# Index tables built from chunk tails: four graph layers on one core of a Trainium2

## The reference

```python
msgs = feature[edge_src]; neigh = segment_sum(msgs, edge_dst)                      # layer 0
h = relu((feature + neigh) @ W1 + b1); out = h @ W2 + b2
scores = einsum('ehd,ehd->eh', q[src], k[tgt]) / sqrt(16) + edges @ We + be        # layer 1
scores = scores * cons[tgt] + relu(distances @ Wd1 + bd1) @ Wd2 + bd2              # softmax over each tgt
agg = segment_sum(x[src], dst); out = self and neighbour products                  # layer 2
agg = segment_sum(edge_weight[:, None] * x[src], dst); out = agg @ W + b           # layer 3
```

## Time and profile before

| | |
|---|---|
| median of three runs | 5493.49 us |
| span of the profiled execution | 5523.1 us |
| first stage, to the barrier | about 0 to 549 us of the span |
| edge batches in it | 49 |
| TensorE busy, whole span | 4522.1 us (82%) |
| VectorE (DVE) busy, whole span | 3190.2 us (58%) |

### The profile page before, as it was taken

How to read it: one execution, slowest core, us unless ns; L and a number is a source line. 1 busy time by engine, 2 the same in 40 slices (tenths; PEclk the granted TensorE clock), 3 DMA queues, 4 the chain that set the end, 5 groups by cost and what they waited for, 6 DMA issues and landing times. The chain is left out here.

```text
span 5523.1 us, 87967 instructions
## 1 busy us (share of the span) xinstructions
PE 4522.1 (82%) x25332; PEld 3171.9 (57%) x25333; DVE 3190.2 (58%) x4531; ACT 1790.6 (32%) x3407; POOL 2040.8 (37%) x1926
## 2 busy tenths in 40 slices
PE   6988665566899968888888888888885499999999
PEld 4656332222788844545555455455543388888888
DVE  6423988877211058988898899989885620000000
ACT  2433367889100030122333344445552410001000
POOL 0320035200000007777777777777775310000000
PEclk9989998988999989999999999999996599999999
DMA  8885567655766643444555566666665566669998
GB/s 182 177 166 123 117 232 277 267 247 241 303 279 279 279 136 81 118 133 139 152 156 169 160 181 185 186 194 195 197 198 149 203 264 279 279 254 297 299 294 264
DMA packets 736811, 1150.50 MB, mean 208 GB/s; under 512 B 310074, under 2 KB 659454, under 8 KB 717888
## 3 DMA queue, kind: packets, MB, share of 16 engines
q1 hardware_dynamic: 461601, 653.45, 34.8%
q10 hardware_dynamic: 211504, 349.71, 18.2%
q0 software_dynamic: 63600, 146.16, 10.6%
HBM read 762.49 MB, written 393.26 MB: 209 GB/s over the span
## 5 line engine op out<-in xcount | busy, mean ns | idle before, releaser
L1518 POOL DMA_INDIRECT at_qg<-q_d,at_slot x1616 | 1676.4, 1037 | 495.8 <-issue 492.4
L713 PE MATMUL bw_ps<-bw_mov,bw_sta 128*128 128x392 bf16 x7056 | 1576.4, 346 | 20.4 <-issue 8.0
L1060 PE MATMUL at_p3t<-tiles,h 128*128 128x256 f32 (+1 forms) x4900 | 1048.5, 376 | 6.2 <-ACT h L915 5.9
L1060 PEld LDWEIGHTS at_p3t<-tiles,h 128*128 128x128 f32 x4900 | 914.0, 191 | 127.1 <-issue 6.1
L1561 PE MATMUL at_psk<-at_kp,at_hot 128*128 x4848 | 615.2, 233 | 357.7 <-DVE at_qg L1639 302.2
L713 PEld LDWEIGHTS bw_ps<-bw_mov,bw_sta 128*128 128x128 bf16 x7056 | 631.8, 101 | 371.3 <-issue 104.4
L1561 PEld LDWEIGHTS at_psk<-at_kp,at_hot 128*128 128x128 bf16 x4848 | 436.3, 100 | 704.7 <-issue 498.1
L713 PE MATMUL ba_ps<-ba_mov,ba_sta 128*128 128x392 bf16 x2352 | 510.4, 363 | 321.3 <-ACT ba_ps L672 126.9
L676 DVE TENSOR_TENSOR ba_mov<-iota,key 128x3136 bf16<-128x3136 f16 x294 | 526.8, 1792 | 131.7 <-PE ba_ps L713 126.9
L713 PEld LDWEIGHTS ba_ps<-ba_mov,ba_sta 128*128 128x128 bf16 x2352 | 241.5, 103 | 590.2 <-issue 474.3
L697 DVE TENSOR_TENSOR bw_sta<-bw_raw,kw 128x1024 bf16<-128x1024 bf16 x882 | 557.4, 687 | 0.0
(11 more groups left out here) (409 smaller groups left out, 3536.1 us busy)
## 6 DMA issues: line engine op xcount, KB each, us to landing
adj_d<-ba_stage ACTq DMA_DIRECT2D x49, 3136.0 KB, 8.9
l0adjt<-adj_d SPq DMA_DIRECT2D x23, 6272.0 KB, 17.3
tiles<-adw_d SPq DMA_DIRECT2D x23, 6272.0 KB, 20.4
tiles<-adj_d SPq DMA_DIRECT2D x22, 6272.0 KB, 17.4
adw_d<-xall ACTq DMA_DIRECT2D x65, 1568.0 KB
adw_d<-bw_stage ACTq DMA_DIRECT2D x33, 1568.0 KB
at_rel<-rel_d SPq DMA_DIRECT2D x101, 512.0 KB
at_qg<-q_d,at_slot POOLq DMA_INDIRECT x1616
```

What stands on the lines that cost most here:

```text
L713: ins = pe.matmul(self.ps[:, bass.DynSlice(place, WCOL)], self.sta[:, k, u // 2, :, u % 2], self.mov[:, u // 2, :, u % 2], start=False, st ...
L1060: ins = pe.matmul(ps_agg[par][:, 0:n * P], h[:, hi, :], moving[hi], start=hi == 0, stop=hi == NB - 1 and not own_term, skip_group_check=ow ...
L1518: pool.indirect_dma_start(out=qg[:, ring, b, :], out_offset=None, in_=q_d[:, :], in_offset=bass.IndirectOffsetOnAxis(ap=slot[:, ring, b:b ...
```

## The change

The three tables are copied from the inputs in DRAM to DRAM by 13 transfers on ACT's queue, ahead of the edge loads there; POOL writes the padding. `rows_d` now has three planes as int32. SP loads the targets once more, and from the last element of each row DVE makes three 0/1 tables, whose products on TensorE count, for each node, the rows that end below it. The windows of all visits come from a second such count. All this stands ahead of batch 0 in TensorE's queue. The gathers of visits and of `KeyTables` follow at once. The visits' keys are made in five groups of up to four columns; `KeyTables.finish` and its stores (now on POOL) follow batches 4 to 7, two more planes and the weights are turned next, and batches 8 to 11 follow. The exact beginnings of the nodes (49 gathers) come last of the index work, and batches 12 to 48 behind them.

```diff
+def index_loads(nc, c, src, dst, edge_weight, x):
 ...
+    x.tails_here = c.L.dma(sp.dma_start(x.tail_row[:, 0:nf, :], dst[0:nf * P * P].rearrange("(g p e) -> p g e", p=P, e=P)))
 ...
+    for k, a in enumerate((dst, src, edge_weight.bitcast(I32))):
+        act.dma_start(c.rows_d[0:whole, k, :], a[0:whole * P].rearrange("(r e) -> r e", e=P)).then_inc(x.s_tables, 16)
 ...
+    for k, a in enumerate((dst, src)):
+        act.dma_start(c.ends_d[0:whole, k * P:(k + 1) * P], a[0:whole * P].rearrange("(r e) -> r e", e=P)).then_inc(x.s_tables, 16)
 ...
+    act.dma_start(c.dst_d[0:whole, :], dst[0:whole * P].rearrange("(r e) -> r e", e=P)).then_inc(x.s_tables, 16)
 ...
+        for k in range(CG):
+            T(pe.matmul(ps[:, 0, 0:NB], over[:, k, :], here[:, k, :], start=k == 0, stop=False))
+            t = T(pe.matmul(ps[:, 0, 0:NB], ones[:], under[:, k, :], start=False, stop=k == CG - 1))
 ...
+        wait(pool, visits)
+        pool.wait_ge(x.s_tables, x.to_tables)
+        wait(pool, x.padded)
+        for i in range(VG):
+            pool.indirect_dma_start(out=vis[:, i, :, :]..., in_=c.rows_d..., ...).then_inc(s_got[i // GV], 16)
 ...
+        keys.places()
+        keys.gather()
 ...
+        edges.batches(0, 4)
 ...
+        for q, i0 in enumerate(range(0, VG, GV)):
+            ve.wait_ge(s_got[q], 16 * n)
+            chain(tensor_tensor d = target - 8 * window, tensor_scalar hi = source >> 7)
+            chain(tensor_scalar o, scalar_tensor_tensor l, scalar_tensor_tensor k)
+            chain(scalar_tensor_tensor o)
+            m = chain(scalar_tensor_tensor k)
+            wait(pe, m)
+            b0, t0 = turn(k, n)
+            b1, t1 = turn(l, n)
+            read(c.key, i0, n, b0, t0, -1.0)
+            read(c.lo, i0, n, b1, t1, 0.0)
+        wait(pe, (V.sem, V.n))
+        edges.batches(4, 8)
+        stored = keys.finish()
+
+        wait(ve, stored)
+        chain(ve.tensor_scalar(hf[:], srcs, 0.5, 1.0 / WCOL, ALU.add, ALU.mult))
         for step in (-0.5, ROUND, -ROUND):
+            chain(ve.tensor_scalar(hf[:], hf[:], step, None, ALU.add))
+        chain(scalar_tensor_tensor dl)
+        chain(scalar_tensor_tensor k2, scalar_tensor_tensor hf)
+        wait(pe, (V.sem, V.n))
+        for what, dest, shift in ((k2, c.kw[:, 0, :], -1.0), (hf, c.lo2, 0.0), (weights, wc, 0.0)):
+            for i0 in range(0, VG, GV):
+                b, t = turn(what[:, i0:i0 + n, :], n)
+                read(dest, i0, n, b, t, shift)
 ...
+        edges.batches(8, 12)
+
+        m = chain(ve.tensor_copy(full_i[:], full[:]))
+        wait(pool, m)
         for j in range(NB):
-            a = V(ve.tensor_scalar(junk[:], heads[:], nodeid[:, j:j + 1], None, ALU.is_lt, ALU.add, accum_out=cnt[:, j:j + 1]))
-            wait(ve, a)
 ...
+            ld = c.Q.dma(pool.indirect_dma_start(out=ends[:, j, :], out_offset=None, in_=c.dst_d[:, :], ...))
+        wait(ve, ld)
+        for j0, j1 in ((0, 25), (25, NB)):
+            chain(ve.tensor_tensor(r, ends[:, j0:j1, :], nodeid[:, j0:j1]..., ALU.is_lt))
+            chain(ve.tensor_reduce(some[:, j0:j1], r, AX.X, ALU.add))
+        m = chain(scalar_tensor_tensor c.rp)
+        wait(pe, m)
         T(pe.matmul(ps[:, 0, 0:NB], c.shift, c.rp[:, 0:NB], start=True, stop=False))
 ...
-        edges.batches(40, EBATCH - 1 - ER)
+        edges.batches(12, EBATCH - 1 - ER)
         edges.last_batches()
         nc.all_engine_barrier()
 ...
+    def finish(self):
+        wait(ve, self.got)
+        m = chain(ve.tensor_copy(rel, ends[:, :, P:2 * P]))
+        wait(pe, m, self.ready)
+        (13 transposes, 8 products on TensorE; DVE reads them into c.index)
+        wait(pe, self.read)
+        (rel, relh, seg, pen, flag, penh on DVE, as L360 to L366)
+        wait(pool, m)
+        (8 stores and kreg_d, pool.dma_start in place of sp.dma_start)
```

More of the change, by code:

```diff
@@ L107, in index_tables @@
[L107 to L119, removed]
@@ L146, in index_tables @@
[L146 to L153, removed]
@@ L154, in index_tables @@
[L154 to L163, removed]
@@ L183, in index_tables @@
[L183 to L186, removed]
+        V(ve.tensor_copy(unit[:], unit_i[:]))
+        V(ve.memset(ones[:], 1.0))
+        V(ve.memset(taken[:], 0.0))
+        V(ve.memset(missing[:], 0.0))
+        V(ve.tensor_copy(firsts[:], c.ident[:].rearrange("p (i u) -> p i u", u=WN)[:, :, 0].unsqueeze(1).to_broadcast([P, UP, WPB])))
@@ new lines, in index_tables @@
+        t = T(pe.matmul(ps[:, 3, 0:NB], c.ones[0:1, :], full[0:1, :], start=True, stop=True))
+        wait(ve, t)
+        chain(ve.tensor_tensor(taken[:, 0:NB], ps[:, 1, 0:NB], unit[:, 0:NB], ALU.mult))
+        chain(ve.tensor_reduce(firstv[:], taken[:].rearrange("p (k u) -> p k u", u=UP), AX.X, ALU.add))
+        chain(ve.tensor_tensor(firstv_i[:], firstv[:], missing[:], ALU.add))
+        chain(ve.tensor_scalar(wl_i[:], firstv_i[:], P - 1, None, ALU.bitwise_and), ve.tensor_scalar(wh_i[:], firstv_i[:], 7, None, ALU.arith_shift_right))
@@ new lines, in index_tables @@
+        chain(ve.tensor_copy(wl[:], wl_i[:]), ve.tensor_copy(wh[:], wh_i[:]))
+        m = chain(ve.tensor_tensor(wover, columns(P, WC), per_column(wl, P), ALU.is_ge), ve.tensor_tensor(where[:], columns(VG, WC), per_column(wh, VG), ALU.is_equal),
+                  ve.tensor_tensor(wunder[:], columns(VG, WC), per_column(wh, VG), ALU.is_gt))
+        wait(pe, m)
+        for k in range(WC):
+            T(pe.matmul(ps[:, 2, 0:VG], wover[:, k, :], where[:, k, :], start=k == 0, stop=False))
+            t = T(pe.matmul(ps[:, 2, 0:VG], ones[:], wunder[:, k, :], start=False, stop=k == WC - 1))
@@ new lines, in index_tables @@
+        V(ve.tensor_scalar(w8[:], c.wt[:], float(WN), None, ALU.mult))
+        chain(ve.tensor_copy(wti[:], c.wt[:]))
+        regs = chain(ve.tensor_scalar(reg[:], wti[:], BANKS, None, ALU.add))
+        keys = KeyTables(nc, c, sb, ps, tid_i, full, hf, k2)
+        keys.places()
+        keys.gather()
+        wait(pool, regs)
+        with nc.allow_non_contiguous_dma(reason="short tables"):
+            S.dma(pool.dma_start(c.first_d.rearrange("(c q) -> q c", q=P), firstv_i[:]))
+            tables_stored = S.dma(pool.dma_start(c.reg_d.rearrange("(i p) -> p i", p=P), reg[:]))
@@ new lines, in index_tables, with turn, read @@
+        edges.batches(0, 4)
+        freed = [None] * 4
+        turned = [0]
+        def turn(what, n):
+            b = turned[0] % 4
+            turned[0] += 1
+            if freed[b]:
+                wait(pe, freed[b])
+            for i in range(n):
+                t = T(pe.transpose(ps[:, b, i * P:(i + 1) * P], what[:, i, :], c.ident[:]))
+            return b, t
+        def read(dest, i0, n, b, t, shift):
+            wait(ve, t)
+            m = min(n * P, NVIS - i0 * P)
+            freed[b] = V(ve.tensor_scalar(dest[:, i0 * P:i0 * P + m], ps[:, b, 0:m], shift, None, ALU.add))
@@ L188, in index_tables @@
+        for j0, j1 in ((0, 25), (25, NB)):
+            r = inside[:, 0:j1 - j0, :]
+            chain(ve.tensor_tensor(r, ends[:, j0:j1, :], nodeid[:, j0:j1].unsqueeze(2).to_broadcast([P, j1 - j0, P]), ALU.is_lt))
+            chain(ve.tensor_reduce(some[:, j0:j1], r, AX.X, ALU.add))
+        m = chain(ve.scalar_tensor_tensor(out=c.rp[:, 0:NB], in0=full[:], scalar=float(P), in1=some[:], op0=ALU.mult, op1=ALU.add))
+        wait(pe, m)
         T(pe.matmul(ps[:, 0, 0:NB], c.shift, c.rp[:, 0:NB], start=True, stop=False))
```

429 lines of the change are left out of this document (202 added, 227 removed).

## The result

The changed kernel takes 5572.99 us (median of four, 5566.10 to 5575.72), the kernel before 5494.47 in the same runs: a ratio of 1.0140, 95% interval 1.0126 to 1.0155. That is 78.5 us slower; 5586 was forecast, from 5545 to 5630. The profiled execution has a span of 5568.7 us at a mean clock of 0.928.

A forecast was written before the change was run, and what follows sets the result against it. The TensorE-ACT hand-over sets 8.72 us a batch, and stops of TensorE's queue add to it. Start 60.0, batches 427.3, waits 136.2, slow clock 10.5, gathers 4, end 0.8 give 638.8, 92 later: 5586 us, range 5545 to 5630.

The forecast's parts named there:

- Start: Beginning of batch 0, behind 13 copies, late edge weights and the counts: at 60 us, from 50 to 70, 27.8 later.
- rival (a): Starved start: the copies hold ACT's queue, batch 0 begins at 85 to 95 us, time 5611 to 5621; chance 0.12.
- First wait: Behind batches 0 to 3, TensorE alternates with DVE over five groups of visits without a batch: 26.5 us, bounds 16 to 35.
- Second wait: `finish`, POOL's nine stores and the second half of the keys, behind batches 4 to 7, no batch beside: 55.7 us.
- Third wait: Exact beginnings: weights split, 49 gathers, comparison, product, 92.3 us, covered only by batches 8 to 11 (38.4): TensorE waits 54.
- slow clock: TensorE behind a stop: a batch takes 10.9 us instead of 8.8, with its beginning 3.5 us; 3 x 3.5 = 10.5 counted.
- Batches: First stage: 49 batches at 8.72 us, 427.3, plus 10.5 for low clock behind stops and 4 for gathers beside batches.
- Sum: All terms to the last bias: 638.8 us against 546.6, 92 later; added to the median 5493.5, this gives 5586.
- Its own criterion: Sign that the prediction is right: everything behind the first stage's barrier unchanged within 10 us.
- (b): Gathers held by DVE: all 49 take 2.0 us instead of 0.96, 51 us more waiting, time 5637; chance 0.03.
- (c): Short waits: quicker DVE operations, stores landing at once; waits 16 + 38 + 45, start at 50, time 5539 to 5549; chance 0.13.
- (d): Batches catch up: loads set the pace, so preloaded batches run faster; with waits overlapping batches, 5440 to 5480; chance 0.05.

## Why the prediction was right, point by point

The mechanism was right: not the length of the index chain but the stops of TensorE's queue set the barrier, and with four batches queued ahead of each wait the waits stick out. That the barrier came within 3.6 us is in part luck: the start was 3.4 us under the forecast and the waits 8.8 over. By the trace after on A:

- Start: 60 forecast, 56.6 measured. Both halves of the argument are seen. The copies delay the weights (41.2 instead of 28.9), POOL's iotas come behind them at 43.8, and the products end at 56. The far bounds (70, and rival (a) with 85 to 95) did not come: the last copy is issued at 40.8 us. The DMA share between 20 and 40 us is 0.93, at 185 GB/s, so the DMA engines were nearly full while the copies ran. The rule of the Trainium skill (DMA: Bandwidth & Descriptors, why a DMA increments its semaphore by 16), by which 1562 rows go to 11 engines, gave as an estimate a start near 70, which did not come; other transfers ran beside, so the traces don't show the rule itself right or wrong.
- First wait: 26.5 forecast, 28.4 measured (94.8 to 123.2). The groups are 6.7 us apart instead of 6.3.
- Second wait: 55.7 forecast, 59.7 measured (160.7 to 220.5). The term that was off is POOL's nine stores: 18.2 us in which DVE waits, instead of 14. The nine issues took 7.5 us, less than the 9 forecast, and the last store took another 10.4 until DVE went on, where the forecast had left 5.
- Third wait: 54 forecast, 56.9 measured (256.0 to 312.9). The chain is as reckoned: from the last turning at 220.5 us to the product's end at 312.9 it is 92.4 us, forecast 92.3 (its terms add up to 92.0). The 49 gathers are 1.25 us apart, and 2.6 us pass from the last issue to DVE's start. What was off is the cover: batches 8 to 11 took 35.5 us. The forecast gave them 38.4, with 3.5 us of slow clock; but the granted clock was at 1.00 from 221 to 256 us, behind the turning of 57 tiles. The sum had taken these 3.5 us from the wait without adding them to the batches.
- Batches: 427.3 + 10.5 + 4 = 441.8 forecast, 440.7 measured (38.2 + 37.5 + 35.5 for the three sets of four, 329.5 for the last 37). The total is right, its parts less so: the first four batches took 3.3 us more than at 8.72 each (4 for gathers forecast), the next eight 3.2, and the last 37 took 6.9, their pace being 8.9.
- Sum: +92 forecast, +95.8 measured for the barrier. The time grew by 78.5, so the forecast of 5586 is 13 us high, and this whole excess and more lies in the step "on the median, 5493.5 + 92", which took everything behind the barrier as unchanged. Its own criterion, 10 us, was missed: some 17 us came back behind the barrier on chip A, for a reason that the runs on other chips don't show.
- Rivals: (b) did not occur, with DVE idle beside the 49 gathers as argued; and beside the 32 first gathers, with DVE busy 7.8 of 20 us, they nearly kept their pace: 1.29 us apart on average, most of them 1.25, the farthest 1.67. (c) and (d) did not occur: no wait was short, and behind the waits batches ran at 8.9 us, not faster, with four batches loaded.

What the prediction did not foresee is that filling the waits would not simply return them. On the chips of the experiments, batches beside stores and DVE work return some 35 us of 47 expected, and batches beside the 49 gathers return nothing.

## What to carry to other kernels

Count how much ready work stands in an engine's queue ahead of each wait, and compare it with the length of the chain that the wait ends; a chain that was free beside 20 queued batches costs 57 us beside four. Before moving work beside a run of indirect gathers, look in a trace of the same chip whether that work keeps its pace beside gathers; in the runs on three of four chips here it did not. A change that moves a barrier is timed best by the barrier itself: its shift was forecast within 4 us, the time within 13.

## What the runs showed of the hardware that was not expected

Chips differ in what an engine gets done beside POOL's gathers. Beside the 49 gathers TensorE is busy 18.6 of 20 us on chip A and 3.3 to 6.8 us on chip C; away from gathers the pace is the same (18.0 to 18.6 of 20 us on both). Each chip was seen at one time only, so whether the chip itself or something else about it then made the difference is not shown. Most of the 1210 to 1280 us by which the kernel before is slower on B, C and D lies in the attention stage, which issues 1616 such gathers: its gathers run from 2067.1 to 4234.9 us on A and from 2123.4 to 5421.3 us on B, 2168 and 3298 us.

The 13 copies from DRAM to DRAM held ACT from 4.4 to 41.4 us. Issuing a copy of 1562 rows took only 0.8 to 1.4 us in five of six cases, and the next issue, of one row, then took 3.4 to 7.4 us; the sixth, 4.3 us, stood itself behind a copy of 1562 single numbers. The two rows at 27.40 and 28.21 us above are such a pair, 0.78 us for 1562 rows and 7.43 for one.
